# Graph network and attention kernel on one core: sixteen edge tiles' target rows added by their gather, attention steps placed between edge tiles, the last row tile handled in pieces, two tiles' outputs by ScalarE and GpSimd

## What is computed

```
gnn:   e   = relu([xn[src], xn[dst]] @ W_kind + b_kind)     8192 edges, sorted by dst; 3 kinds: 256, 1280, the rest
       ex  = exp(e @ W_a + b_a  -  max over the edges of the same dst)
       z   = sum(ex * xn[src]) / sum(ex)                     per node
       new = relu([xn, z] @ W_node + b_node)                 2 kinds of node: rows 0..127 (HN), rows 128..511 (ON)
mix:   q, k = elu(.) + 1, v: linear attention of 16 heads; out = (q (k^T v)) / (q . sum k) @ w_proj + b
x1 = x + new + mix
mlp:   h = gelu(quant(norm(x1)) @ quant(w1) + b1);  out = x1 + quant(norm(h)) @ quant(w2) + b2
```

## Time and profile before

| | us |
|---|---|
| three runs | 641.26, 641.54, 640.56 |
| median | 641.26 |
| the profiled execution, its own time | 637.06 |
| its span | 635.2 |
| TensorE (PE) busy | 598.5 |
| VectorE (DVE) busy | 505.2 |
| ScalarE (ACT) busy | 280.6 |
| GpSimd (POOL) busy | 219.1 |
| DMA packets and bytes | 44910, 171.43 MB |

### The profile page before, as it was taken

How to read it: one execution, slowest core, us unless ns; L and a number is a source line. 1 busy time by engine, 2 the same in 40 slices (tenths; PEclk the granted TensorE clock), 3 DMA queues, 4 the chain that set the end, 5 groups by cost and what they waited for, 6 DMA issues and landing times.

```text
span 635.2 us, 8449 instructions
## 1 busy us (share of the span) xinstructions
PE 598.5 (94%) x2858; PEld 465.9 (73%) x2860; DVE 505.2 (80%) x843; ACT 280.6 (44%) x467; POOL 219.1 (34%) x177
## 2 busy tenths in 40 slices
PE   5999999999999999969999999999999989999845
PEld 3788888888888887758888888888886327887422
DVE  6868961659859798968969978899989996648885
ACT  3335324443435253546454445754435994412201
POOL 3000040277636747236627735255110000214320
PEclk9999999999999999979999999999999999999987
DMA  8852563699999999788979959699984213895514
GB/s 326 345 188 97 208 225 124 215 376 415 417 407 356 390 389 398 299 314 299 366 292 319 409 202 382 223 329 325 393 278 181 85 27 135 295 256 188 155 39 127
DMA packets 44910, 171.43 MB, mean 270 GB/s; under 512 B 5572, under 2 KB 5956, under 8 KB 37700
## 3 DMA queue, kind: packets, MB, share of 16 engines
q1 hardware_dynamic: 20016, 86.19, 36.3%
q0 software_dynamic: 21744, 79.90, 35.0%
q10 hardware_dynamic: 3108, 4.81, 2.5%
HBM read 154.08 MB, written 16.80 MB: 269 GB/s over the span
## 4 chain that ended last, share of the span: by engine, by line
PE 56%; DVE 14%; issue 11%; DMA 8%; ACT 7%; POOL 3%; DVEq 0%; another core or an unknown queue 0%; POOLq 0%; ACTq 0%
PE bank_low L1638 15%; PE bank_low L1640 15%; PE bank_low L1639 15%; DMA w_raw<-in_wt 4%; DMA gathered_dst<-edge_tables,dst_row 2%; ACT w_hi L710 2%; ACT hot_hi L834 2%; DVE w_lo L1012 2%; PE bank_high L1640 2%; PE bank_high L1638 1%; PE bank_high L1639 1%; DVE gathered_rows L1191 1%; PE bank_high L1870 1%; PE bank_low L1993 1%; DMA edge_tables<-stage 1%
## 5 line engine op out<-in xcount | busy, mean ns | idle before, releaser
L1638 PE MATMUL bank_low<-w_hi,xT_hi 128*128 128x512 f32 x476 | 188.5, 396 | 6.3 <-ACT bank_low L741 5.4
L1640 PE MATMUL bank_low<-w_hi,xT_lo 128*128 128x512 f32 x476 | 186.1, 391 | 0.0
L1639 PE MATMUL bank_low<-w_lo,xT_hi 128*128 128x512 f32 x476 | 186.0, 391 | 0.0
L623 POOL DMA_INDIRECT gathered_rows<-edge_tables,src_row x68 | 99.2, 1459 | 156.6 <-DVE gathered_rows L1197 112.9
L710 ACT ACTIVATE w_hi<-w_raw 128x2048 fp32r<-128x2048 f32 x49 | 93.9, 1916 | 121.9 <-DMA w_raw<-in_wt 70.5
L1012 DVE TENSOR_TENSOR w_lo<-w_raw,w_hi 128x2048 fp32r<-128x2048 f32 x49 | 112.0, 2290 | 32.9 <-ACT w_hi L710 32.4
L1638 PEld LDWEIGHTS bank_low<-w_hi,xT_hi 128*128 128x128 f32 x476 | 89.9, 189 | 25.6 <-ACT bank_low L741 5.8
L1640 PEld LDWEIGHTS bank_low<-w_hi,xT_lo 128*128 128x128 f32 x476 | 89.8, 189 | 19.1
L1639 PEld LDWEIGHTS bank_low<-w_lo,xT_hi 128*128 128x128 f32 x476 | 90.0, 189 | 18.2
L1191 DVE TENSOR_TENSOR gathered_rows<-gathered_rows,gathered_dst 128x1024 f32<-128x1024 f32 x68 | 82.9, 1219 | 10.3 <-DMA gathered_dst<-edge_tables,dst_row 6.5
L623 POOL DMA_INDIRECT gathered_dst<-edge_tables,dst_row x68 | 80.8, 1189 | 20.7 <-issue 20.7
(11 more groups left out here) (304 smaller groups left out, 882.2 us busy)
## 6 DMA issues: line engine op xcount, KB each, us to landing
w_raw<-in_wt SPq DMA_DIRECT2D x54, 1024.0 KB
edge_tables<-stage SPq DMA_DIRECT2D x32, 256.0 KB
bias_bc<-in_bias_rows ACTq DMA_DIRECT2D x16, 256.0 KB
x_in<-in_x SPq DMA_DIRECT2D x4, 512.0 KB, 9.4
xn_scratch<-xn SPq DMA_DIRECT2D x4, 512.0 KB, 6.5
node_top<-stage SPq DMA_DIRECT2D x8, 256.0 KB
mix_out<-stage SPq DMA_DIRECT2D x8, 256.0 KB
xn_raw<-xn_scratch SPq DMA_DIRECT2D x4, 512.0 KB, 7.9
```

Of the source, the lines that this page charges most:

```text
L623: pool.indirect_dma_start(dest, None, table_d[0:nodes, :], bass.IndirectOffsetOnAxis(ap=index[:, t:t + 1].bitcast(U32), axis=0), compute_o ...
L1638: pe.matmul(dest, lh, rh, start=start and i == 0, stop=False, skip_group_check=True)
L1639: pe.matmul(dest, lh, rl, start=False, stop=False, skip_group_check=True)
L1640: last = pe.matmul(dest, ll, rh, start=False, stop=last_one, skip_group_check=True)
```

## The change

- `ADDED_HERE` holds only tiles 0 to 51. For tiles 52 to 67 GpSimd issues the second gather two tiles later, after the source rows have landed, with an addition into the same slot (the branch for `u not in ADDED_HERE`, which is there before too). VectorE leaves out L1191 for them. `dst_bc` waits for 52 additions, not 68.
- `TILES` has other numbers. `STEPS_AT` names attention steps by chunk, place and number of tiles done, so that they can stand between two tiles; `add_kq` and `spread_ks` are placed by it too.
- The tables of TensorE, `HOT_BEFORE`, `LO_ON_ACT` and a few places of `hi_half` and `lo_half` are changed.
- At the start row tile 0 of `x` is loaded and normalised in two halves, and the transposes of the first half start on their own.
- In the tail the last product of the last row tile is made in two pieces of 256 columns (`bottom(3, 1)`, `bottom(3, 2)`), its rows are finished in three pieces, and its left half is quantised by VectorE, its right half by ScalarE and VectorE. `turn_in` (transposes) is taken out of `up`. The filler products (14 now) stand before `turn_in(3)`. `norm_in(3)` and `quantise_in(3)` stand before `hidden(2)`; `round_in(0)` stands right after `quantise_in(0)`. For the second and third row tile ScalarE scales the output (`scale_out`) and GpSimd adds x2 (`add_out`).

More of the change, by code:

```diff
@@ L290, in sem @@
         return nc.alloc_semaphore(name)
-    x_loaded = [sem(f"x_loaded{m}") for m in range(MT)]
+    x_loaded = [sem(f"x_loaded{m}") for m in range(MT + 1)]
     small_loaded = sem("small_loaded")
@@ L400, in build @@
     o_psum = sem("o_psum")
-    o_done = sem("o_done")
+    o_read = [sem(f"o_read{j}") for j in range(MT)]
+    o_done = [sem(f"o_done{j}") for j in range(MT)]
     out_stored = sem("out_stored")
@@ L900, in _ @@
             hot_tiles(t, t + 1)
-            if t == HOT_BEFORE[ON1, 1][1] + 12:
+            if t == HOT_BEFORE[ON1, 1][1] + 15:
                 hi_half(HN1, 1)
@@ L1393, in hot_hh, with attention @@
                 hot_source(t)
-        def attention(c, place):
-            for what in SCALE_AT.get((c, place), "").split():
+        def attention(c, place, tiles=0):
+            for what in STEPS_AT.get((c, place, tiles), "").split():
                 a = int(what[1])
-                if what[0] == "k":
-                    for j in range(4):
-                        add_kq("q", a, j)
+                if what[0] in "kq":
+                    add_kq(what[0], a, int(what[2]))
+                elif what[0] == "s":
+                    spread_ks(a)
                 elif what[0] == "l":
@@ L1411, in _ @@
             edge_work(c, 0)
-            if c in (V0, V1):
-                for j in range(4):
-                    add_kq("k", int(c == V1), j)
             attention(c, 2)
@@ L1960, in up, with keep_warm @@
                     last.then_inc(qT_psum, 1)
+        def up(j):
+            m = ORDER[j]
             pe.wait_ge(qT_done, 2 * j + 2)
+            if Y_BANK[j] == 1:
+                pe.wait_ge(bot_evac, 6)
             for k in range(KT):
-                last = pe.matmul(bank[5][:, 0:H], q8T[m][:, k, :], w1T[:, k, :], start=k == 0, stop=k == KT - 1)
+                last = pe.matmul(bank[Y_BANK[j]][:, 0:H], q8T[m][:, k, :], w1T[:, k, :], start=k == 0, stop=k == KT - 1)
             last.then_inc(y_psum, 1)
+        def keep_warm():
+            pe.wait_ge(bot_evac, 7)
+            for _ in range(FILL):
+                pe.matmul(bank[2][:, :], zeros[:, :], iota[:, :], start=True, stop=True)
         def down(j):
@@ L2013, in _ @@
         bottom(3, 1)
+        bottom(3, 2)
+        turn_in(2)
+        down(1)
         up(2)
-        down(1)
+        keep_warm()
+        turn_in(3)
         up(3)
-        for _ in range(FILL):
-            pe.matmul(bank[0][:, :], zeros[:, :], iota[:, :], start=True, stop=True)
         down(2)
```

139 lines of the change are left out of this document (85 added, 54 removed).

## The result

The changed kernel is slower. On the first chip its median is 650.9 us (649.9 to 652.5, four runs) against 641.4 (640.6 to 643.4, four runs): ratio 1.0146, 95% interval 1.0114 to 1.0178. Run again later, beside other runs (e5), it was 1.0228 (1.0159 to 1.0298). I had forecast 638.8 with 632.5 to 644. Its profiled execution took 652.5 us, span 650.7, against 637.1 and 635.2; single executions of the kernel before lay between 633 and 647 in all groups, so the 15.5 us between the two profiles are more than the 9.5 between the medians. The profiles say where the time sits, the ratios how much it is.

A forecast was written before the change was run, and what follows sets the result against it. TensorE, busy 94% of the span, was taken as the bound, four waits summing to 17 us. Gains of 0.7 (maxima), 0.6 (one-hot), 0 (start) and 1.2 (tail) made 2.5: 641.3 to 638.8 us, range 632.5 to 644.

The forecast's parts named there:

- the arrival of the last edge tile and of TensorE at the turned maxima: At PR1's end: last tile done at 462, TensorE there at 456.1, waiting some 6 us; ON1 starts 0.7 us earlier.
- V0: TensorE's 5.4 us wait for a PSUM bank seed goes by earlier kbuf additions: gain 6.3 us, bounds 5 and 7.
- The start: Halved first load and normalised row of x: taken as nothing, bounds -0.3 and +0.6 us.
- T5: Three tiles instead of two ahead of T5's first low half: 0 to 2.5 us new stall, taken as swallowed.
- The sixteen rows: Adding gathers for 16 tiles: 1.4 us more DMA time each, 22 us against 16.2 free; work ends at 459.4.
- rival B: At PR1's maxima: additions starve the edges' end, each us behind 464.5 costs one; sign a wait above 9; chance 0.20.
- The tail: Last row tiles: shorter VectorE chain and full clock, against 1.7 for round_in(0) and 0.8 for outputs: +1.2, bounds -2 and +3.
- Full clock for the last transposes: In the tail: fill matmuls in the wait let transposes and `up` run at full clock, 0.4 us gained each.
- rival C: In the tail: GpSimd's additions hold the last power and outputs, -2 instead of +1.2, giving 642.0 us; chance 0.12.
- The one-hot stage: Seven groups of low one-hot tiles on ScalarE instead of eight: +0.6 us, bounds -0.7 and +1.6; moved high half nothing.

The follow-up runs named there:

- e5: The changed kernel again, unaltered, beside other runs, against the kernel before: 653.2 us, ratio 1.0228.
- e7: The kernel before with the V0 steps alone (k00 and k01 added after the third of five K0 tiles, two tiles at V0): 634.9 us, ratio 0.9936.
- e17: The kernel of e7 again, on another chip, against the kernel before: 635.2 us, ratio 0.991.
- e16: The kernel of e4 again (kernel before, adding gathers for tiles 52 to 67 at their old places): 647.7 us, ratio 1.0186.
- e1: The changed kernel with the start undone (row tile 0 of x loaded, normalised and transposed whole): 649.7 us, ratio 1.0158 to the kernel before.
- e2: The changed kernel with VectorE adding the target rows of all 68 tiles again: 650.4 us, ratio 1.0151 to the kernel before.
- e4: The kernel before with one part alone: tiles 52 to 67 get target rows by an adding gather, at their old places: 649.7 us, ratio 1.017.
- e13: As e4, but the second gather of tiles 52 to 67 copies instead of adding, same order and waits: 639.9 us, ratio 1.0015 to the kernel before.
- e6: The kernel before with the changed tail alone: 643.6 us, ratio 1.0055.
- e3: The changed kernel with turn_in(0) behind the next product, bottom(2, 0), instead of ahead of it: 655.8 us, ratio 1.0238 to the kernel before.
- e11: The kernel of e7 with the changed tail, but round_in(0) and turn_in(0) at their old places: 633.9 us, ratio 0.9889 to the kernel before.
- e18: The kernel of e11 again, on another chip, against the kernel before: 635.1 us, ratio 0.9921.
- e15: The kernel of e11 with the changed one-hot shares (HOT_BEFORE, LO_ON_ACT, places of the last halves): 638.0 us, ratio 0.9986 to the kernel before.

## Why the prediction was wrong

The failed step is the arrival of the last edge tile and of TensorE at the turned maxima. The prediction had the last tile done at 462, TensorE there at 456.1 and a wait of some 6 us. In the profile the last tile was done at 474.2, TensorE was there at 464.6 and waited 9.7, and half clock behind the wait, which no term held, took 1.9 more. Three premises of that step failed: a start 6.6 us earlier, a stage packed without holes, and tiles at new places that nothing else delays. By its terms:

- **V0.** Right in its mechanism and near in its size. I forecast 6.3 (the working, 285.6 to 279.0, is 6.6); the profiles of e7 and e17 show 7.4 and 5.8 from K0 to the first product of `kbuf`, the ratios 4 to 6 us, part of it lost again behind PR0 in e17. In the changed kernel 1.64 us came back at K1, which I had not looked at:

```profile
278.78 0.50 PE L1690 MATMUL bank_low<-w_hi,xT_hi 128*128 128x512 f32 x1 [0.50 <-ACT bank_low L760]
297.47 0.47 PE L1690 MATMUL bank_low<-w_hi,xT_hi 128*128 128x512 f32 x1 [1.64 <-ACT bank_low L760]
```

- **The start.** I took it as nothing, with -0.3 at worst, and priced two issues and an instruction. It costs 3 to 4. What I left out is what half rows do to the transfers queued beside them. The first products of the timeline below came 1.33 us later (11.79 against 10.46), and with TensorE's granted clock at 0.50 from 12 to 20 us this had become 3.75 at the second transposes. The changed kernel's timeline:

```profile
11.79 2.04 PE L1724 MATMUL bank_low<-w_hi,xT_hi 128*128 128x512 f32 x4 [2.46 <-ACT xT_hi L735]
15.77 0.80 PE L1729 MATMUL bank_low<-w_lo,xT_hi 128*128 128x512 f32 x1 [1.93 <-DVE xT_lo L1057]
```

- **T5.** The stall was forecast at 0 to 2.5 and was 1.7; that it would be swallowed was wrong. At K0 the shift is still 5.7: VectorE's chain there moved with TensorE.

```profile
149.96 0.50 PE L1690 MATMUL bank_low<-w_hi,xT_hi 128*128 128x512 f32 x1 [1.71 <-DVE w_lo L1048]
```

- **The sixteen rows.** The price was right (2.67 forecast from the earlier trace rows, 2.66 in e16, against 1.41 plain), and so was the sum of work. The end wasn't: 459.4 for a start 6.6 us earlier with every hole filled. The stage began 1.8 us later instead, 8.4 in all, and holes of 4.5 us stayed (share 0.95 over 370 to 460), most of it from 410 to 420, where five slots were full, GpSimd waited 15.1 us and VectorE 6.3 for the sums of q. 459.4 + 8.4 + 4.5 = 472.3, which is where the last tile was summed. I worked this sum out afterwards, and it is rough: the share goes above 1.00 in several windows, to 1.05. VectorE's timeline:

```profile
464.17 1.23 DVE L1233 SCALAR_TENSOR_TENSOR gathered_rows<-gathered_rows,wa_bc 128x1024 f32<-128x1024 f32 x1 [1.96 <-DMA gathered_rows<-edge_tables,dst_row]
...
468.95 1.23 DVE L1233 SCALAR_TENSOR_TENSOR gathered_rows<-gathered_rows,wa_bc 128x1024 f32<-128x1024 f32 x1 [2.83 <-DMA gathered_rows<-edge_tables,dst_row]
...
472.28 1.23 DVE L1233 SCALAR_TENSOR_TENSOR gathered_rows<-gathered_rows,wa_bc 128x1024 f32<-128x1024 f32 x1 [1.39 <-DMA gathered_rows<-edge_tables,dst_row]
```

The prediction's own sign for rival B, a wait above 9, is met: 9.7, and 9.2 and 9.1 in e1 and e5. It is B in its mechanism, with a second cause that no rival named: five tiles behind ON1's low half (e2). By rival B's price, one us for each us behind 464.5, a last tile at 474.2 gives 651.0, and the median is 650.9. That agreement is partly luck, as the price leaves out the start, T5, the half clock and the tail, and e4 has the loss with the wait at the maxima at only 2.9. The fit for one transfer on the page "DMA: Bandwidth & Descriptors" of the Trainium skill (Anatomy of one DMA) has a fixed part and a part by bytes, and no term for an addition. The runs differ with it there: between e13 and e16, at the same bytes, the addition costs 1.2 us a tile more.

- **Half clock behind the wait.** Rival B counted the wait alone. The first nine products behind it ran at 1.2 GHz (granted clock 0.50 from 475 to 479 us), 1.9 us more:

```profile
474.29 1.11 PE L1840 MATMUL bank_high<-ident,running_min 128*128 128x128 f32 x4 [9.69 <-DVE running_min L1248]
475.05 0.78 PE L1690 MATMUL bank_low<-w_hi,oT_hi 128*128 128x512 f32 x1
```

- **The tail.** Forecast +1.2, measured in e6 as -2.3 by the length and -3.5 by the ratio, both below my bound of -2. The 1.7 that I charged for `round_in(0)` is VectorE's wait of 1.19 for ScalarE. That TensorE's transposes now stand ahead of a product which needed no rounding I did not charge at all. Taking this back alone brings nothing (e3), taking back both makes the tail as fast as the old one (e11, e18), and which part `round_in(0)` has by itself is not shown. The changed kernel's transposes:

```profile
594.22 0.61 PE L2013 MATMUL bank_high<-ident,q 128*128 128x128 bf16 x8 [2.74 <-DVE q L1598]
```

Part of this wait is not the tail's own: these transposes stand 46.7 us behind the first product of z here and 47.3 in e5, but 45.0 in e6, where the low half of the z stage is at its old place (see e15).

Full clock for the last transposes did not come either: they took 0.76 and `up` 1.03, the granted clock of 634 to 650 was 0.56. GpSimd's additions took 1.25 each (forecast 1.1), and the last power was not late:

```profile
636.47 2.53 POOL L684 TENSOR_TENSOR hbuf<-hbuf,x 128x512 f32<-128x512 f32 x2
640.16 0.59 POOL L677 TENSOR_TENSOR small<-small,nhalf 128x1 f32<-128x1 f32 x1 [1.16 <-DVE small L1613]
```

The page "GPSIMD Engine Reference" of the Trainium skill (Elementwise) gives 4.5 us for an addition of 2048 elements, divided by four an estimate of 1.1; the trace is near it, with 1.25.

So rival C did not occur.

- **The one-hot stage.** Forecast 0.6, the profile has 0.65 (13.64 to 12.99). I put the moved halves at nothing. In e15 the same edit costs 3 to 4 us in the length of the tail, 2.5 of them seen in VectorE's wait for the additions into x: the load of these waits behind a weight load in SyncE's queue.

What stays open: why half rows at the start cost the DMA engines a quarter of their rate; how much of the 650.9 the place of the five tiles and the gathers each take, since they overlap; whether GpSimd's longer issue of an adding gather has a part; and the moved low half by itself, which only traces show.

## What to carry to other kernels

Work that is taken from an engine with spare time and given to the DMA engines was a loss here, where their share went from 0.82 to 1.00: price it in engine time, add the holes that the slots enforce, and start the sum from the arrival that the profile has, not from one that another part of the change is hoped to give. For each transfer or transpose that is split or moved earlier, read what stands behind it in its queue; for each step moved later, read what waits for it there, as the loads for x waited behind one low half (e15). Change one step at a time: the V0 step alone is worth 4 to 6 us and was hidden under four others.

## What was not expected of the hardware

An adding gather of 0.52 MB takes 2.66 us of the sixteen DMA engines, a plain one 1.41, in the same stretch. Two loads of 256 KB in place of one of 512 at the start brought the rate of all queues from 408 to 308 GB/s over four microseconds (314 to 339 in the changed kernel, e5 and e2). GpSimd took a median of 1.54 us to issue an adding gather and 0.95 for the plain one in its place (e13). Eighteen executions of the kernel before on one chip lay between 635 and 647 us (mean granted clock 0.984 in the fastest, 0.976 in the slowest), so gains under 3 us were not resolved by four runs of each.
